# Another order of three steps inside the slots that interleave one block's layer norm with the next block's heads, in the gated delta attention of a two-layer hybrid model

## The reference, cut to what matters

```python
q = silu(_dwconv_causal(x @ Wq, qconv_w, qconv_b)).reshape(b, t, H, D)
k = silu(_dwconv_causal(x @ Wk, kconv_w, kconv_b)).reshape(b, t, H, D)
v = silu(_dwconv_causal(x @ Wv, vconv_w, vconv_b)).reshape(b, t, H, D)
a = sigmoid(x @ Wa + ba).reshape(b, t, H, D)
beta = sigmoid(x @ Wb + bb)
o = _delta_scan(q, k, v, a, beta)
mu = jnp.mean(o, axis=-1, keepdims=True)
var = jnp.mean(jnp.square(o - mu), axis=-1, keepdims=True)
o = (o - mu) * rsqrt(var + LN_EPS) * ln_g + ln_b
g = sigmoid(x @ Wg).reshape(b, t, H, D)
return (o * g).reshape(b, t, H * D) @ Wo
```

## Time and profile before

| | |
|---|---|
| median of 3 runs | 3222.84 us (3212.23 to 3224.44) |
| profiled execution | 3215.73 us |
| its span, first to last instruction | 3214.0 us |
| mean granted TensorE clock | 0.840 |
| busy: PE, DVE, ACT, POOL | 2507.8, 1760.9, 1218.1, 1379.3 us |
| the three interleaved phases, slots 1 to 8 | from 1706.96, 2059.94 and 2416.42 us, some 105 us each |
| the tail, slots 1 to 8 | from 2761.04 us, some 54 us |

### The profile page before, as it was taken

The page is one execution under the profiler, slowest core; times in us unless marked ns, Lnnn a source line. Parts: engine busy times, 40 slices in busy tenths (PEclk is TensorE's granted clock), DMA queues, the critical chain, the costliest instruction groups (busy, mean ns, idle before and its releaser), DMA issues. The chain is left out here.

```text
span 3214.0 us, 45378 instructions
## 1 busy us (share of the span) xinstructions
PE 2507.8 (78%) x16766; PEld 2058.1 (64%) x16778; DVE 1760.9 (55%) x3323; ACT 1218.1 (38%) x2736; POOL 1379.3 (43%) x1063
## 2 busy tenths in 40 slices
PE   6799846998896979776678847785778757659798
PEld 4688725888573758665566746665667646526677
DVE  2422365223455543476686586766686687345533
ACT  2333232332331424354345633464345534213233
POOL 0454313553201005447682496438672587210054
PEclk9799977999897979887678958797669857879899
DMA  0210002100000014032222332213232232010050
GB/s 30 79 59 20 0 17 79 56 23 0 17 1 18 1 50 146 14 104 94 96 80 95 100 101 96 76 66 124 67 118 69 88 126 80 27 48 1 35 161 13
DMA packets 121568, 198.73 MB, mean 62 GB/s; under 512 B 60048, under 2 KB 94752, under 8 KB 116256
## 3 DMA queue, kind: packets, MB, share of 16 engines
q1 hardware_dynamic: 121376, 196.21, 19.0%
HBM read 192.38 MB, written 3.81 MB: 61 GB/s over the span
## 5 line engine op out<-in xcount | busy, mean ns | idle before, releaser
L444 PE MATMUL PS<-XP_moe,WP_moe 128*128 128x512 f32 x1536 | 355.8, 392 | 30.4 <-POOL WP_moe L518 28.6
L444 PEld LDWEIGHTS PS<-XP_moe,WP_moe 128*128 128x128 f32 x1536 | 290.0, 190 | 91.2 <-issue 28.7
L2107 DVE SCALAR_TENSOR_TENSOR XT<-M_delta,CW_delta,XT 128x256 f32<-128x256 f32 x576 | 251.4, 495 | 108.8 <-ACT M_delta L1975 72.1
L1792 PE MATMUL PS<-ident,XT 128*128 128x128 f32 x512 | 114.3, 406 | 251.1 <-DVE XT L2165 235.9
L1792 PEld LDWEIGHTS PS<-ident,XT 128*128 128x128 f32 x512 | 91.9, 210 | 270.5 <-DVE XT L2165 131.9
L1741 PE MATMUL PS<-XP_delta,X 128*128 128x268 f32 (+1 forms) x1024 | 243.8, 391 | 7.3 <-DMA X<-in_L_attn_b_heads 7.2
L558 DVE TENSOR_TENSOR HF_moe<-SG_moe,PS 128x512 f32<-128x512 f32 x128 | 88.0, 688 | 265.2 <-ACT SG_moe L495 265.1
L1741 PEld LDWEIGHTS PS<-XP_delta,X 128*128 128x128 f32 x1024 | 192.2, 190 | 56.0 <-issue 11.4
L524 POOL TENSOR_TENSOR HP_moe<-HF_moe,HP_moe 128x512 fp32r<-128x512 f32 x128 | 163.5, 1291 | 138.3 <-ACT HP_moe L488 138.3
L1019 ACT ACTIVATE PR_attn<-PS,NM_attn 128x256 f32<-128x256 f32 (+1 forms) x384 | 135.2, 419 | 225.2 <-DVE NM_attn L1079 225.2
L1256 PE MATMUL PS<-XP_rffn,UW_rffn 128*128 128x512 f32 x816 | 194.8, 396 | 4.8 <-POOL UW_rffn L1212 4.6
(11 more groups left out here) (314 smaller groups left out, 5735.7 us busy)
## 6 DMA issues: line engine op xcount, KB each, us to landing
M_delta<-gram_delta SPq DMA_DIRECT2D x32, 2304.0 KB, 8.5
X<-in_L_attn_b_heads SPq DMA_DIRECT2D x64, 512.0 KB, 3.3
W_moe<-in_L_ffn_w SPq DMA_DIRECT2D x48, 512.0 KB, 4.7
CB_rffn<-routes_rffn SPq DMA_DIRECT2D x20, 512.0 KB, 23.1
XN<-in_L_attn_b_outs SPq DMA_DIRECT2D x16, 512.0 KB, 3.7
F_delta<-in_L_attn_b_outs SPq DMA_DIRECT2D x4, 2048.0 KB, 8.5
W_rffn<-in_L_ffn_tiles SPq DMA_DIRECT2D x4, 1536.0 KB, 12.1
W_rffn<-in_L_ffn_tiles SPq DMA_DIRECT2D x2, 2304.0 KB, 26.8
```

Of the source, the lines that this page charges most:

```text
L444: last = nc.tensor.matmul(PS[:, 2 * (g % 2) + i, :], up_w(qw, r, i, k, m), XP[qx][:, k, n * NB:(n + 1) * NB], start=(k + step == 0), stop= ...
L1792: last = nc.tensor.transpose(PS[:, 6 + r % 2, i * P:(i + 1) * P], W[:, B * h:B * (h + 1), :], core.ident[:])
L2107: nc.vector.scalar_tensor_tensor(TMP[:, r, i], RAW[:, r, i, :, tau:tau + BT], CW[:, i, h, tau:tau + 1], TMP[:, r, i], ALU.mult, ALU.add).t ...
```

## The change

Three steps change their place inside a slot; no instruction is added, taken away or changed. On ACT `square` comes first in the slot, ahead of the evacuation of head A. On PE `variance` comes right behind head A, ahead of the two `project`. On POOL `power` comes ahead of head B's `tap`. In phase 0 there is no norm and nothing moves. In the tail there are no heads, so that only PE's swap of `variance` and `project` is left.

```diff
@@ heads_and_norm on POOL
                         tap(n, 2 * k - 2)
                         if k > 1:
                             scale_key(n, 2 * k - 3)
-                        tap(n, 2 * k - 1)
                     if n and k < NW:
                         power(n - 1, k)
                     if n < NBLK:
+                        tap(n, 2 * k - 1)
                         scale_key(n, 2 * k - 2)
@@ heads_and_norm on PE
                     if n < NBLK:
                         head(n, 2 * k - 2)
+                    if n and k < NW:
+                        variance(n - 1, k)
                     if n:
                         project(n - 1, 2 * k - 2)
                         project(n - 1, 2 * k - 1)
-                    if n and k < NW:
-                        variance(n - 1, k)
                     if n < NBLK:
                         head(n, 2 * k - 1)
@@ heads_and_norm on ACT
                 for k in range(1, H // 2 + 1):
+                    if n and k < NW:
+                        square(n - 1, k)
                     if n < NBLK:
                         evacuate(n, 2 * k - 2)
                         if k > 1:
                             silus(n, 2 * k - 3)
-                    if n and k < NW:
-                        square(n - 1, k)
-                    if n < NBLK:
                         evacuate(n, 2 * k - 1)
                         silus(n, 2 * k - 2)
```

## The result

| | before | changed |
|---|---|---|
| median | 3220.35 us (4 runs, 3212.23 to 3224.44) | 3167.01 us (4 runs, 3158.17 to 3171.0) |
| ratio, 95% interval | | 0.9838 [0.9814, 0.9862] |
| profiled execution | 3215.73 us | 3158.17 us |
| mean granted clock | 0.840 | 0.842 |

The changed kernel is 1.6% faster, 53 us between the medians. 3173 us was forecast.

A forecast was written before the change was run, and what follows sets the result against it. PE was taken to bound the kernel, with waits for power and square; 37.4 us from three phases and 9.2 from the tail, 46.6 in all, gave 3169.1 or 3176.2 us, so 3173 was taken, range 3161 to 3190.

The forecast's parts named there:

- The two waits and their real cost: PE's waits in an interleaved slot: ahead of spread 1.43 us, ahead of variance 0.41, together 1.84 off 13.58.
- ACT's added delay: Interleaved slot: square first makes head A's evacuation 0.25 us late, passed on to head A's tap and taps.
- The ring through DVE and POOL: Interleaved slot: power, gated and taps close within PE's 11.74 us, with 1.3 us to spare ahead of spread and variance.
- rival (1): Interleaved phases: DVE becomes the bound, 12.6 us a slot, 28.7 us gained in all, about 3191 us; chance 0.07.
- PE's swap in the phases: Interleaved slot: variance right behind head A, at 4.45 us, with project at 5.36, as part of the 1.84 us gain.
- Slot 8: Last slot of a phase: has no group and keeps its length; DVE catches up in it.
- The sum: Slots 2 to 7 and slot 1 give 12.5 us a phase, 37.4 for three; with the tail 46.6 us.
- The tail: Slots without heads: spread starts 1.38 us sooner in each of six, perhaps 0.9 in the first, 9.2 us in all.
- Rival (3): Interleaved slots: the clock falls to 1.2 GHz; one whole phase costs 83 us, near 3256 us, slower; chance 0.02.
- The rule on shared access: Interleaved slot: by the skill, head B's taps would wait for power's end, 0.2 of 1.3 us to spare, sum unchanged.

The follow-up runs named there:

- the two kernels with more work: The changed kernel with two more instructions like power on POOL (3187.64 us), or three copies ahead of gated on DVE (3192.91 us), in the interleaved phases.
- the one with more copies: The changed kernel with three unread copies of 128x512 ahead of gated's first instruction on DVE in the interleaved phases: 3192.91 us, ratio 0.9943.

## Why the prediction was right

**The two waits and their real cost.** It held. The waits read as 1.25 and 0.24 us, and the steps behind them said 1.43 and 0.41. POOL's part alone took 1.51 us off a slot, ACT's part alone 0.50. The steps were the better reading, and still a little short: `spread` to `centre` fell from 0.99 to 0.89 us too once nothing held `spread` up. The slot was laid out at 11.74 us and came to 11.56; 0.10 of the difference is that step, and another 0.10 is the step from `variance` to what follows, for which I had taken 0.91 and which is 0.81. The steps behind `project` (1.81 for 1.72) and behind head B (3.60 for 3.67) nearly cancel.

**ACT's added delay.** The times that it was to give came true, but by another cause. Head A's evacuation does start later, 2.13 us into the slot against 1.97 before and 2.22 laid out. But the second of its instructions on the projections (L1973) starts at 2.88 before and 2.89 after, and head A's `tap` at 4.27 and 4.28: the delay never got to POOL or to `shift`, as the prediction had it. With ACT's part alone (slot from 1751.99) `shift` stays at 7.85 us:

```profile
1754.12 0.57 ACT L1973 ACTIVATE XT<-PS,CB_delta,CW_delta 128x256 f32<-128x256 f32 x1
1756.26 0.56 POOL L1622 TENSOR_SCALAR XT<-M_delta,CW_delta,CB_delta 128x256 f32<-128x256 f32 x1 [4.21 <-ACT M_delta L1975]
1759.84 0.15 DVE L2202 TENSOR_SCALAR RT_delta<-PS 128x4 f32<-128x4 f32 x1
```

With POOL's part alone (slot from 1748.12), where ACT's order is the old one, `shift` comes at 8.14 all the same, behind a `tap` that takes 0.84 us:

```profile
1752.40 0.84 POOL L1622 TENSOR_SCALAR XT<-M_delta,CW_delta,CB_delta 128x256 f32<-128x256 f32 x1 [2.69 <-ACT M_delta L1975]
1753.34 3.00 DVE L2107 SCALAR_TENSOR_TENSOR XT<-M_delta,CW_delta,XT 128x256 f32<-128x256 f32 x7 [0.45 <-POOL XT L1622]
1756.26 0.15 DVE L2203 TENSOR_SCALAR RT_delta<-PS 128x4 f32<-128x4 f32 x1
```

So the 0.25 us that I laid on `shift` was put down to ACT and is 0.28 us of a slower `tap`: it runs beside the first two `taps` of head A, which come later in the shorter slot. The prediction looked only at what POOL might cost DVE, not at what DVE might cost POOL. That the two sizes agree is luck.

**The ring through DVE and POOL.** `power` was laid out from 8.35 to 9.37 us and ran from 8.38 to 9.40, as near as that by the luck just named. `gated` was to start at 2.50 and starts at 2.52. The room of 1.3 us was read off as 1.1 by the two kernels with more work. So rival (1), DVE as the bound, was refuted, with about 1.1 us between it and the forecast rather than the 0.1 that the bare sum of DVE's pieces suggested: the waits between the taps do shrink, to 0.45 us in one place for head A in the changed kernel and to none for that head in the one with more copies.

**PE's swap in the phases.** I described it as a part of the gain and did not ask what it gives alone. It gives nothing: `shift` stands behind head A's `taps` on DVE until 8.1 us, and `variance` behind `project` is done by 7.1 (with ACT's and POOL's parts, without PE's). By itself it costs 2%. What it gives is the tail, by `variance` getting ahead of `project`: 1.52 us a slot, 1.38 laid out, and some 10 us in all (from the first `spread` to the start of the last `project` 51.55 us before and 41.44 after).

**Slot 8.** I had it unchanged; it grew by 0.43 us (from `spread` to gram 14.52 before, 14.95 after), since `gated` and with it `taps` of head A now come later there and `project` waits for it ahead of head B. It is a small term that I got wrong, and it took back 1.3 us of the phases' gain.

**The sum.** From the first `spread` of a phase to gram it took 110.33, 111.33 and 110.58 us before and 97.69, 97.34 and 97.07 after: 12.6, 14.0 and 13.5 us less, with slot 8's loss in it, where 12.5 was laid out for each. Slots 2 to 7 gave 2.03 us each in place of 1.84, for the steps named above; slot 1 gave 0.87, 2.22 and 1.75 us in place of 1.43. That is 40.1 us for the phases. The tail gave 10.1 us up to the last `project`, where 9.2 was laid out, and 1.8 more in the last `project` itself, which ran at a granted clock of 0.50 before (3.78 us) and of 1.00 after (1.99 us); that term nobody had laid out. Together they are 52 us of the 57.6 between the two profiled executions. The rest lies in code that the change doesn't touch, and is not the prediction's merit or fault. The stretch from gram to the first `centre` of the next phase (scan and updates) took 230.1, 231.9 and 227.9 us before, 227.7, 232.2 and 227.2 after, and 227.5, 235.3 and 227.0 in the repeat of the changed kernel. The 2.4 us between the first two of before and changed arise in one place: PE's updates between the two halves of the scan ran at a granted clock of 0.51 for five microseconds before, and at 1.00 after. What decides that from execution to execution wasn't tried.

**The clock as a rival.** Rival (3) did not happen to this kernel. It did happen, on a small scale, to PE's part alone. In the changed kernel PE has no wait left in slots 1 to 7, and its clock read 1.00 through slots 3 to 7 of the first phase. In slot 8 it waits 0.27 us for `gated`.

**The rule on shared access.** Where `power` runs beside a `taps` instruction (1738.62 to 1739.64, and `taps` from 1739.30), that instruction took its usual 0.48 us and was not held up; the Trainium skill (SBUF — State Buffer, "Who interferes with whom") would have it wait. But in slot 8, where `tap` on POOL was started under the second instruction of `gated`, `tap` took 1.23 us in place of 0.56:

```profile
1791.27 0.75 DVE L2214 SCALAR_TENSOR_TENSOR V_delta<-V_delta,LN_delta,KQ_delta 128x512 f32<-128x512 f32 x1
1791.46 1.23 POOL L1622 TENSOR_SCALAR XT<-M_delta,CW_delta,CB_delta 128x256 f32<-128x256 f32 x1 [1.83 <-ACT M_delta L1975]
```

The DVE instruction ended at 1792.02, and 0.56 us and a little more from there is 1792.69, the end of `tap`. By that rule, this row agrees. Head A's `tap` in the steady slots lies between the two: it starts at 1734.52 beside two `taps` instructions that end at 1734.62 and 1735.01, and is held by 0.28 us, where waiting for the one would give 0.10 and for both 0.49. It was so in slots 3 to 7 of each phase, and nowhere in the phases before. What makes one pair wait and another not wasn't tried.

## What to carry to other kernels

Where several in-order engines pass work round in a ring, lay one period out on a common clock, with each engine's queue as it stands, and compare for each wait when its input was written with when its producer was allowed to start: a producer that stands behind unrelated work that itself waits for the slow engine (here `power` behind head B's `tap`) costs the whole period. Price a wait by the distance between starts with and without it, not by the idle time shown. Move a consumer forward only together with its producer: `variance` ahead of `project` cost 2% alone and nothing in the phases with `square` moved as well. Ask of every engine whose work comes later what it will now run beside: a `tap` that came to run beside `taps` took 0.84 us in place of 0.56, and `shift` came that much later. Then test each part alone, as one of three gave nothing in the stage for which it was argued.

## What the runs showed of the hardware

With PE's part alone the granted clock fell once in every slot, behind the wait ahead of `variance` and `variance`'s own single-column matmuls: 0.66 over the next five microseconds, 1.7 us lost. In the steady slots that wait is 1.97 us. In slot 1 it is 1.05 us, and the clock fell there too:

```profile
1713.15 1.05 PE L1859 MATMUL PS<-ONES_delta,A_delta 128*128 128x1 f32 x8 [1.05 <-ACT A_delta L2003]
```

```profile
1714.70:1718.20 3.50, 3.50 (x10) 2.73 (x9) 0.73 (x3) 0.00 (x0) 0.00 (x0) 0.51 0.03 11
```

Waits of 1.25 us ahead of `spread` in the kernel before, of 0.51 ahead of `variance` in the kernel with more on DVE, and of 0.70 and 1.34 in each slot of the tail before left the clock at 1.00. A wait of 1.05 us went with a fall and one of 1.34 with none, so the length of the wait alone does not tell; how much of it is owed to the light matmuls behind the wait wasn't tried. Six matmuls that nobody reads, in the wait, paid for themselves: 1.7 us a slot, 1.1% of the kernel that had the wait.

Unchanged code moves by several microseconds between executions: the stretch from gram to `centre` behind the second phase took 231.9 and 232.2 us in before and changed, at a mean granted clock of 0.68, and 235.3 in the repeat of the changed kernel, at 0.66. That is as much as one of the smaller parts of this change is worth. So the parts were told apart by the slots, whose steady ones repeated to 0.01 us in nearly every case, and the times only confirmed them.
